# Mixing the values of eight heads at a time in two row and four column groups of TensorE, with paired transposes and the two biases made ahead of wq's low parts

## What is computed

```python
# grouped (layers 0, 2)
q = (rmsnorm(x) * norm_w) @ wq                     # 16 heads x 32
k, v = cond @ wk, cond @ wv                        # 4 heads x 32, 64 keys
attn = softmax(q k^T / sqrt(32))                   # head (g, r) uses k, v of group g
x = x + (attn v) @ wo
# masked (layers 1, 3)
attn = softmax((x Wq)(c Wk)^T / 8 + col_bias)      # 16 heads x 64
x = x + (attn (c Wv)) @ Wo + bo
```

## Time and profile before

| | |
|---|---|
| time, median of 3 runs | 1560.08 us (1559.84 to 1560.52) |
| the profiled execution | 1558.53 us, span 1556.7 us |
| PE busy | 1522.4 us, 98% |
| DVE busy | 1004.1 us, 64% |
| POOL busy | 881.2 us, 57% |
| ACT busy | 750.1 us, 48% |
| PE on the chain that ended last | 90% |
| transfers | 170.62 MB, 110 GB/s over the span |

### The profile page before, as it was taken

The page is one execution under the profiler, slowest core; times in us unless marked ns, Lnnn a source line. Parts: engine busy times, 40 slices in busy tenths (PEclk is TensorE's granted clock), DMA queues, the critical chain, the costliest instruction groups (busy, mean ns, idle before and its releaser), DMA issues.

```text
span 1556.7 us, 22870 instructions
## 1 busy us (share of the span) xinstructions
PE 1522.4 (98%) x8224; PEld 1233.7 (79%) x8224; DVE 1004.1 (64%) x1661; ACT 750.1 (48%) x1317; POOL 881.2 (57%) x809
## 2 busy tenths in 40 slices
PE   7995999999999999999999999999999999999998
PEld 7985887788778877788778877887778877887787
DVE  5774658766676657765776657665776577665664
ACT  4564566335733465336633574346533563256331
POOL 0054467556764676467745675467745775568431
PEclk9997999999999999999999999999999999999999
DMA  9998572122321331132212232143113231222201
GB/s 338 340 402 297 205 256 88 35 79 89 109 61 34 133 116 48 35 117 72 100 41 71 95 109 61 31 135 116 42 41 94 87 99 51 65 95 88 55 1 54
DMA packets 109071, 170.62 MB, mean 110 GB/s; under 512 B 25504, under 2 KB 58784, under 8 KB 102944
## 3 DMA queue, kind: packets, MB, share of 16 engines
q1 hardware_dynamic: 104976, 151.59, 29.7%
q10 hardware_dynamic: 3824, 17.04, 2.7%
q0 software_dynamic: 160, 0.53, 0.1%
HBM read 117.48 MB, written 51.65 MB: 109 GB/s over the span
## 4 chain that ended last, share of the span: by engine, by line
PE 90%; POOL 4%; DVE 2%; DMA 1%; ACT 1%; issue 1%; SPq 1%; ACTq 0%; DVEq 0%; POOLq 0%
PE OB L379 16%; PE OB L381 15%; PE OB L380 15%; PE SB L379 10%; PE SB L381 9%; PE SB L380 9%; PE TB L508 5%; PE MX L546 4%; POOL xhl L1299 2%; PE MX L508 2%; POOL prob L1264 1%; PE SB L487 1%; DMA s_fm<-prob 1%; PE OB L434 1%; PE OB L431 1%
## 5 line engine op out<-in xcount | busy, mean ns | idle before, releaser
L1270 POOL TENSOR_TENSOR prob<-prob,small 128x512 f32<-128x512 f32 x256 | 278.7, 1091 | 288.9 <-DVE small L1072 288.9
L1264 POOL TENSOR_TENSOR prob<-prob,small 128x512 f32<-128x512 f32 x128 | 136.3, 1065 | 142.0 <-DVE small L1047 142.0
L1053 DVE SCALAR_TENSOR_TENSOR prob<-SB,aux 128x512 f32<-128x512 f32 x128 | 88.0, 688 | 199.0 <-PE SB L381 199.0
L379 PE MATMUL SB<-foldM,xhl 128*128 128x512 f32 x512 | 203.0, 396 | 4.4 <-POOL xhl L1299 2.5
L379 PE MATMUL OB<-pT,foldN 128*128 128x512 f32 x512 | 204.9, 400 | 0.0
L381 PE MATMUL SB<-foldM,xhl 128*128 128x512 f32 x512 | 199.8, 390 | 0.0
L380 PE MATMUL OB<-pT,foldN 128*128 128x512 f32 x512 | 199.8, 390 | 0.0
L381 PE MATMUL OB<-pT,foldN 128*128 128x512 f32 x512 | 199.8, 390 | 0.0
L380 PE MATMUL SB<-foldM,xhl 128*128 128x512 f32 x512 | 199.4, 389 | 0.0
L795 ACT ACTIVATE prob<-prob 128x512 f32<-128x512 f32 x128 | 80.5, 629 | 172.8 <-DVE prob L1059 172.0
L1047 DVE TENSOR_REDUCE small<-prob 128x8 f32<-128x512 f32 x128 | 87.4, 683 | 109.8 <-ACT prob L804 109.8
(11 more groups left out here) (136 smaller groups left out, 3833.7 us busy)
## 6 DMA issues: line engine op xcount, KB each, us to landing
prob<-in_wkvM_dram SPq DMA_DIRECT2D x32, 512.0 KB, 8.4
ring<-s_fm SPq DMA_DIRECT2D x64, 256.0 KB, 5.4
ring<-s_fn SPq DMA_DIRECT2D x128, 128.0 KB, 2.6
out_dram<-x ACTq DMA_DIRECT2D x15, 1024.0 KB, 3.9
s_fm<-prob SPq DMA_DIRECT2D x16, 512.0 KB, 7.7
wraw<-in_wqG_dram SPq DMA_DIRECT2D x8, 1024.0 KB, 8.4
s_fn<-x SPq DMA_DIRECT2D x16, 512.0 KB, 5.5
ring<-in_xT_dram SPq DMA_DIRECT2D x32, 256.0 KB, 3.2
```

The lines of the kernel that those rows point to most:

```text
L379: pe.matmul(out, a_hi, b_hi, start=start, stop=False)
L1053: dve.scalar_tensor_tensor(out=own, in0=bank, scalar=M_SCALE, in1=row, op0=ALU.mult, op1=ALU.add).then_inc(S["biased"], 1)
L1264: pool.tensor_tensor(own, own, hmax[u % 2].unsqueeze(2).broadcast_to([P, HH, KEYS]), ALU.subtract).then_inc(S["evac"], 1)
L1270: pool.tensor_tensor(own, own, rsum[u % 2].unsqueeze(2).broadcast_to([P, HH, KEYS]), ALU.mult).then_inc(S["normed"], 1)
```

## The change

- **Mixing.** `mixing(it, ph, m)` now handles eight heads, for `m` in 0 and 1: eight calls, each with 64 rows (one head's keys) and 32 columns (one head's width). Row group `a` (partitions 64a to 64a+63) holds a head of key/value group 2m+a and writes bank TB (a = 0) or MX (a = 1); column group `i` writes partitions 32i to 32i+31. `vG` holds the values once for each row group, with no zeros, and is filled by two transfers instead of four.
- **Copied scores.** So that heads i of groups 2m and 2m+1 stand beside each other, ACT's copy of the grouped scores writes `prob` with a pattern of 2 x 4 x 64 elements instead of a run of 512.
- **Transposes** go in pairs, to TB and MX; `pF` has four buffers. Each output bank pair gives two blocks of `oT`, so `ot_hi` and `ot_lo` come in pairs too.
- **Orders** of PE, ACT, DVE and POOL in phases 1 and 2 are rewritten for this. The first mixing of phase 2 moves ahead of the first masked scores. The exponential of step 7 moves ahead of `xb_hi`, `norm(1, 6)` ahead of `xb_lo`.
- **Start.** POOL makes both biases first, and wq's low parts after them. The clearing of `vG` goes.
- The count `evac` is split in two (POOL's `evac`, DVE's `shifted`), with no new wait.

```diff
             def mixing(it, ph, j, first):
-                pe.wait_ge(S["pt_hi"], 8 * (k - 1) + 2 * j + 2)
-                if j == 0:
-                    pe.wait_ge(S["ld_vg"], 64 * (it + 1))
-                ...
-                for o in range(2):
-                    half = slice(64 * o, 64 * o + 64)
-                    last = pe.matmul(MX[half, :], vG[:, 2 * j + o, half], pF[:, o, :], start=True, stop=True)
+            def mixing(it, ph, m):
+                pe.wait_ge(S["pt_hi"], 8 * (k - 1) + 4 * m + 4)
+                if m == 0:
+                    pe.wait_ge(S["ld_vg"], 32 * (it + 1))
+                for i in range(4):
+                    for a in range(2):
+                        rows = slice(64 * a, 64 * a + 64)
+                        g = 2 * m + a
+                        last = pe.matmul(t_bank(ph, a)[32 * i:32 * i + 32, :], vG[rows, g * HD_G:(g + 1) * HD_G], pF[rows, i, :],
+                                         start=True, stop=True)
                 last.then_inc(S["mixed"], 1)
...
             def grouped_grouped(it, first):
                 scores(it, 1, 0, first)
+                transposes(it, 1, 4, first)
+                transposes(it, 1, 5, first)
+                scores(it, 1, 1, first)
+                out_part(it, 1, 0, 0)
+                scores(it, 1, 2, first)
+                transposes(it, 1, 6, first)
+                transposes(it, 1, 7, first)
+                out_part(it, 1, 0, 1)
+                scores(it, 1, 3, first)
+                out_part(it, 1, 1, 0)
+                scores(it, 1, 4, first)
+                out_part(it, 1, 1, 1)
+                mixing(it, 1, 1)
+                for u in range(5, STEPS):
+                    scores(it, 1, u, first)
                 transposes(it, 2, 0, first)
+                transposes(it, 2, 1, first)
+                out_part(it, 1, 2, 0)
                 out_part(it, 1, 3, 0)
                 out_part(it, 1, 2, 1)
+                transposes(it, 2, 2, first)
+                transposes(it, 2, 3, first)
                 out_part(it, 1, 3, 1)
+                mixing(it, 2, 0)
...
             def copied(it, ph, u):
-                act.activation(prob[ph][:, u % 4, (u // 4) * HALF:(u // 4 + 1) * HALF], SB[u % 2][:, :], ACT.Copy)
+                own = prob[ph][:, u % 4, (u // 4) * HALF:(u // 4 + 1) * HALF]
+                act.activation(own.rearrange("p (i a k) -> p a i k", a=2, k=KEYS),
+                               SB[u % 2][:, :].rearrange("p (a i k) -> p a i k", a=2, k=KEYS), ACT.Copy)
...
             for lp in range(PAIRS):
                 if lp:
                     pool.wait_ge(S["bias_b"], lp)
-                    for c in range(DC):
-                        ws_lo(0, c)
...
+            for c in range(DC):
+                ws_lo(0, c)
             pool.wait_ge(S["idented"], 4)
```

More of the change, by code:

```diff
@@ L186, in t_bank @@
         def t_bank(ph, t):
-            return MX if ph in (0, 3) and t % 2 else TB
+            return MX if t % 2 else TB
         def kg_part(it, r):
@@ L249, in vg_load @@
                 for a in range(2):
[L250 to L253, removed]
+                    sp.dma_start(vG[64 * a:64 * a + 64, :], sVG[it // BATCH, it % BATCH]).then_inc(S["ld_vg"], 16)
             for n in range(4):
@@ L453, in q_bound @@
                 for c in range(DC):
[L454 to L457, removed]
+                    if ph == 1 and c in (1, 2):
+                        transposes(it, 1, 2 * c - 2, first)
+                        transposes(it, 1, 2 * c - 1, first)
+                    elif ph == 1 and c == DC - 1:
+                        mixing(it, 1, 0)
                     elif c == DC - 1 and not first:
@@ L493, in transposes @@
                 pe.wait_ge(S["normed"], 8 * (k - 1) + 4 * (t // 4) + 4)
[L494 to L497, removed]
+                if first and ph == 1 and t < 2:
+                    pe.wait_ge(S["ev_d" if t else "ev_a"], 2 * MASKED)
                 elif ph == 0:
@@ L652, in masked_grouped @@
-                mixing(it, 2, 3, first)
+                out_part(it, 2, 0, 0)
+                scores(it, 2, 1, first)
+                transposes(it, 2, 4, first)
+                transposes(it, 2, 5, first)
+                out_part(it, 2, 0, 1)
+                scores(it, 2, 2, first)
+                transposes(it, 2, 6, first)
+                transposes(it, 2, 7, first)
+                out_part(it, 2, 1, 0)
+                scores(it, 2, 3, first)
+                out_part(it, 2, 1, 1)
@@ L653, in masked_grouped @@
+                mixing(it, 2, 1)
+                scores(it, 2, 4, first)
+                scores(it, 2, 5, first)
+                out_part(it, 2, 2, 0)
+                scores(it, 2, 6, first)
                 out_part(it, 2, 2, 1)
-                scores(it, 2, STEPS - 1, first)
+                scores(it, 2, 7, first)
                 transposes(it, 3, 0, first)
@@ L823, in part_hi, with xb_hi @@
                 act.activation(fold_part(i, 0), ring[:, i % 4, :], ACT.Copy).then_inc(S["fold_hi"], 1)
-            def xb_hi(it, ph):
+            def xb_hi(it, ph, chunks=range(DC)):
                 k = 4 * it + ph
-                for c in range(DC):
+                for c in chunks:
                     act.wait_ge(S["xnew"], 4 * (k - 1) + c + 1)
@@ L917, in body @@
                         exp(it, 2, s - 2)
-                ot_hi(2 * it + 1, 3)
+                    if s == 2:
+                        pt_hi(it, 2, 4)
+                        pt_hi(it, 2, 5)
+                    elif s == 3:
+                        pt_hi(it, 2, 6)
+                        pt_hi(it, 2, 7)
+                    elif s == 5:
+                        ot_hi(2 * it + 1, 2)
+                        ot_hi(2 * it + 1, 3)
                 exp(it, 2, STEPS - 2)
@@ L1044, in evac @@
                     dve.wait_ge(S["copied"], 16 * it + 8 * ph + u + 1)
-                    if not (first and ph == 0 and u < 2):
-                        dve.wait_ge(S["evac"], 8 * k + u - 1)
+                    if ph == 0 and u < 2 and not first:
+                        dve.wait_ge(S["shifted"], 16 * it + u - 1)
+                    elif ph == 1 or u >= 2:
+                        dve.wait_ge(S["evac"], 8 * (2 * it + ph) + u - 1)
                     dve.reduce_max(hmax[u % 2], own, AX_X).then_inc(S["maxed"], 1)
@@ L1120, in body @@
                 ot_lo(2 * it, 0)
+                ot_lo(2 * it, 1)
                 q_lo(it, 1)
```

135 lines of the change are left out of this document (65 added, 70 removed).

## The result

The changed kernel takes 1511.38 us (median of 4 runs, 1509.78 to 1513.75), the kernel before 1560.05 in runs on the same chip: a ratio of 0.969, with a 95% interval from 0.967 to 0.971. That is 48.7 us less. The forecast was 1517, with a range from 1505 to 1533.

What follows compares the result with a forecast made beforehand. PE, busy 98% of the span, was taken to bound the kernel. From the profiled 1558.5: - 34.4 + 2 + 2.5 - 13.0 = 1515.6; the median of the runs is 1.5 above, so 1517 us, range 1505 to 1533.

Steps and rivals of the forecast that it cites:

- The mixing: Grouped phases: 64 mixings costing 74.4 us become 32 of 1.20 plus 0.05 stagger, 40.0 us; 34.4 saved.
- The step that carried it: In the new mixing, two row groups and four column groups run at once: two passes of 0.43 plus 0.15.
- The stagger: Spread of the starts of a mixing's eight calls: taken as 0.05 us per mixing, at most 0.15.
- The rival with pairs of column groups: Each mixing: only two column groups run at once, four passes instead of two; 27 us more, 1544; chance 0.09.
- the rival with queue order: Each mixing: records served in queue order, 3.0 us more per mixing, +96, 1613; chance 0.05.
- The pairs of transposes: 64 pairs in grouped phases: 0.94 against 2 x 0.44 each, at most 3.8 us lost; 2 taken.
- Operands inside phase 1: Before phase 1's scores: paired operand work on ACT and DVE stays hidden behind PE's work, by 0.4 us.
- The passage: Phase 1 to phase 2, 8 times: 0.7 us of waits saved, new wait of 1.1; 2.5 us lost in all.
- Queued behind that exponential on ACT: Passage: ACT's copies end at 10.7, PE reaches `mixing(2, 0)` at 9.6, so it waits 1.1 us.
- The rival with larger waits at every passage: Each of 16 grouped phases exposes 0.7 us of new waits instead of 0.15; 9 us more, 1526; chance 0.07.
- The start: Biases first on POOL remove ACT's 11.99 us wait, all behind moves up 12.0; 13.0 us saved, bounds 9 to 14.5.
- Both corrections: Start: up to 2.5 us more from work formerly at half clock; against it, transfers with 12 us less to drain.

Runs made afterwards that it cites:

- The doubled calls: The changed kernel with the eight calls of each mixing issued twice in a row; 1538.95 us.
- the two calls: The changed kernel with only two of the eight calls of each mixing, six heads of eight left unmixed; 1510.48 us.
- both orders of the banks: The changed kernel, and the same with the mixing's loops exchanged: four calls to TB, then four to MX, instead of in turn; the latter 1511.69 us.
- the biases alone: The kernel before with one edit: POOL makes both biases ahead of all low parts of wq, mixing as before; 1546.27 us, ratio 0.991.
- the mixing alone: The changed kernel with the biases' edit undone: wq's low parts again between the biases on POOL; 1524.07 us, ratio 0.977 to the kernel before.
- the earlier copies: The changed kernel with transposes for heads 2 and 3 ahead of the last output piece and ACT's copies ahead of the last exponential; 1510.12 us, ratio 0.968.
- the later sums: The kernel with the earlier copies, and VectorE's sums of step 7 moved behind the low parts of the new x; 1508.76 us, ratio 0.968.

## Why the prediction was right

**The mixing** (34.4 predicted). A mixing costs 1.21 instead of the 1.25 assumed, so the term is 74.4 - 32 x 1.21 = 35.7. The step that carried it, that two row groups and four column groups compose, was the one without a row in the trace before. The doubled calls show it (27.6 us for eight more calls in each of 32 mixings, two passes), and the two calls show its reverse (about 1 us for six fewer). The stagger was taken as 0.05 from 0.01 between neighbours, and is 0.04. The rival with pairs of column groups wanted 1.9 from mixing to product, and the rival with queue order 4; it is 1.02.

That last rival was also what the Trainium skill would give (TensorE: Matmul & The Clock Gate, Part 3, "The mechanism"). The trace doesn't agree with strict program order of records: with two calls, the second record in TB starts at 707.72, behind the first one in MX at 707.27. With eight calls the rows don't name the call, but if each set holds one record of each, the first call's second record starts behind the eighth's first, in both orders of the banks. The same section draws tiles that start about 4 ns apart, with a span of one matmul plus that stagger; in kind this is what is seen, and here it is 7 ns.

**The pairs of transposes** (2 lost). Wrong in size, by all of it. The timeline of PE:

```profile
711.10 0.60 PE L507 MATMUL TB<-ident,prob 128*128 128x128 f32 x4
711.53 0.60 PE L507 MATMUL MX<-ident,prob 128*128 128x128 f32 x4
711.89 0.36 PE L375 MATMUL SB<-kG,foldM 128*128 128x256 f32 x1
712.09 0.28 PE L376 MATMUL SB<-kG,foldM 128*128 128x256 f32 x1
```

The pair costs 712.09 - 711.10 - 0.12 = 0.87, twice a single one. The 0.94 of the earlier trace rows came from one place, and not a typical one; the median over that kernel's pairs is 0.88 by the same reading.

**Operands inside phase 1** (hidden). No wait of PE stands there, and the strided copy costs 597 ns, what the copy without a stride cost. The term holds.

**The passage** (2.5 lost). PE loses 0.71 + 0.23 + 0.19 = 1.13 each time. The passage before has to be read in the same way, up to the second product behind each wait. The one behind the second wait stands here in the timeline of PE before:

```profile
761.71 0.39 PE L380 MATMUL SB<-foldM,xhl 128*128 128x512 f32 x1
```

With the earlier trace rows the waits before are 760.48 - 759.45 - 0.23 - 0.44 = 0.36 and 761.71 - 760.71 - 2 x 0.23 = 0.54, together 0.90 and not the 0.71 of the prediction. So 0.23 x 8 = 1.8 are lost. The wait stands where it was foretold and names the engine that was foretold; it is 0.7, not 1.1. But the step "Queued behind that exponential on ACT are thus exactly the copies that `mixing(2, 0)` waits for" gives only the place. With those copies out of the way the loss is the same. What is behind them, VectorE's work on the new x, is as late, and that was not in my chain. The rival with larger waits at every passage wanted 9 us more; it is less than the forecast's 2.5.

**The start** (13.0 saved). ACT's 11.99 went whole. From the start to the first mixing it was 12.3 in the pair of executions compared. With the biases alone it was 11.2. Over all executions that were profiled, the first mixing comes at 221.7 and 223.6 with the old order, and at 208.3 to 213.6 (ten executions, mean 210.7) with the new one: 12.0. The first product of x with wq comes 13.8 earlier, but 1.5 of that is lost again before the first mixing, so little came back in the end of what the half clock of the earlier trace rows had cost. The new order has a stretch of its own at 0.83 of full clock (start and end, length, busy time of PE, PEld, DVE, ACT, POOL, clock, DMA share, GB/s):

```profile
140.00:150.00 10.00, 9.14 (x50) 7.79 (x51) 3.30 (x6) 2.85 (x6) 2.17 (x2) 0.83 1.05 411
```

Within it the clock stood at the lower level (0.50, 1.2 GHz) from 142 to 144, after PE had idled 1.75 up to 140.86. The transfers that I set against the gain fill this stretch (share 1.05, 411 GB/s). Both corrections together are worth 0 to 0.3; they were not told apart.

**The sum.** Terms as measured: 35.7 - 0 - 1.8 + 12.3 = 46.2, where the profiled executions differ by 1558.5 - 1509.8 = 48.7. So 2.5 us stay without a term of the prediction. Half of it shows in the traces: from 230 us on, the mean distance between two products of 512 columns that follow each other without a wait is 0.2284 before and with the biases alone, and 0.2281 in the changed kernel and with the mixing alone. Over the 4524 products behind the first mixing that is some 1.3 us. It goes with the new mixing and its orders; why the products are closer is open. The rest is within the reading of a mixing before (1.15 from starts rounded to 0.01, taken 64 times), which is uncertain by 0.02, or 1.3 us.

Held against the profiled execution, where the forecast was 1515.6 and the time 1509.8, it was 5.8 too high: 1.3 from the mixing, 2.0 from the transposes, 0.7 from the passage, less 0.7 from the start, and 2.5 without a term. The mechanisms of the two large terms were right, and each came out within 1.3 us of its size. Four of the five errors have the same sign, so the total is not close by errors that cancel.

## What to carry to other kernels

When small matmuls use a part of the array, count passes: here eight plain float32 calls of 64 rows and 32 columns, in different row and column groups and issued in a row, cost the passes of one call together and 7 ns for each further call. So heads should be gathered until the array is full, even if, as here at no cost, operands have to be copied with a stride. This pays where TensorE bounds the kernel, as it does here at 98%. A wait's label names what came last; before taking that work forward, look at what each engine behind it is doing, because in a passage where VectorE is busy for 7 us on end, as here, a wait is moved and not removed. A wait of one engine for a whole stage of another (two biases, here), if only its first part is needed or it could have been made earlier, can be worth as much as a third of a change in the main loop.

## What the runs showed of the hardware

- The plain float32 calls of the mixing leave two records each, and the records of eight calls stand in two sets, the second 0.43 to 0.45 behind the first. Calls from the same row group next to each other or in turn make no difference (1.02 from mixing to product in both).
- VectorE's subtraction of two tiles in SBUF took 1.48 and 1.53 beside POOL's work (2.92 for two), and 1.53 and 0.68 (2.13 for two) when POOL stood idle for the second; the same operation with one operand in a bank took 0.64 to 0.68 in both. POOL's multiplication took 1.50 beside it and 1.04 elsewhere. The three long ones end 0.55 after POOL's operation beside them has ended: at 733.71 after 733.16 and at 735.16 after 734.61 with the earlier copies, at 734.23 after 733.68 with the later sums. The Trainium skill has a rule for it (SBUF — State Buffer, "SBUF: two separate sides"): VectorE with two operands in SBUF and GpSimd share one pair of ports, which one of them holds for a whole instruction. The rows agree with it (these three distances of 0.55, less than the 0.68 that one such operation takes alone); no run here separated the ports from other causes.
- The start varies by several us from one execution to the next: the first mixing came between 208.3 and 213.6 in ten executions with the same order on POOL, while the changed kernel's two profiled executions agree to 0.05 us from each mixing to the next. Differences under some 3 us in this kernel are better read from mixing to mixing than from the total.
